# Moving the feed-forward steps in the hand-made order of an attention kernel: one turn, one linear and one statistics step each get another place

## The reference

```python
x = _layernorm(x + attention(x, w_qa, q_a_ln_w, w_qb, w_kva, kv_a_ln_w, w_kvb, w_o))   # 16 heads, causal
x = _layernorm(x + (einsum('bsi,oi->bso', x, weight * scale_weight[:, None]) + bias))
```

## Time and profile before

| | before |
|---|---|
| median of 3 runs | 1750.34 us (1749.48 to 1751.75) |
| the profiled execution | 1751.75 us |
| its span, first to last instruction | 1750.1 us |
| PE / PEld / DVE / ACT / POOL busy | 97 / 79 / 79 / 64 / 55 % |
| mean granted TensorE clock | 0.993 |

### The profile page before, as it was taken

One profiled execution on the slowest core, in us unless ns is written; L12 is line 12 of the kernel. 1 busy time (PEld: TensorE's weight loads), 2 busy tenths in 40 slices (PEclk: granted clock), 3 DMA queues, 4 the chain that ended last, 5 costly groups with the idle time before them and its releaser, 6 DMA issues.

```text
span 1750.1 us, 27869 instructions
## 1 busy us (share of the span) xinstructions
PE 1700.8 (97%) x8729; PEld 1390.7 (79%) x8729; DVE 1375.5 (79%) x2502; ACT 1122.8 (64%) x2133; POOL 963.3 (55%) x901
## 2 busy tenths in 40 slices
PE   7997899999999999999999999999999999999987
PEld 5565688888888888888888888888888888888554
DVE  3555787888888887878888888888888988888763
ACT  3553466675667576666667666766667766776763
POOL 3320355565565555555566555555655655665874
PEclk9998999999999999999999999999999999999999
DMA  6977221212311322223211412123113121113121
GB/s 200 344 284 244 63 79 58 82 55 87 130 55 61 115 67 67 80 66 128 79 55 49 133 55 91 55 70 127 58 55 127 45 65 43 43 43 108 56 91 67
DMA packets 111864, 165.28 MB, mean 94 GB/s; under 512 B 13488, under 2 KB 84144, under 8 KB 109424
## 3 DMA queue, kind: packets, MB, share of 16 engines
q1 hardware_dynamic: 105376, 124.03, 22.0%
q10 hardware_dynamic: 1728, 24.12, 3.3%
q0 software_dynamic: 4624, 15.47, 2.7%
HBM read 100.14 MB, written 63.44 MB: 93 GB/s over the span
## 4 chain that ended last, share of the span: by engine, by line
PE 88%; DVE 3%; DMA 3%; POOL 2%; issue 2%; ACT 2%; SPq 0%; DVEq 0%; ACTq 0%; POOLq 0%
PE rows L1406 35%; PE bank L1439 7%; PE bank L1436 7%; PE bank L1437 7%; PE rows L1469 6%; PE rows L1371 5%; PE bank L1469 3%; PE bank L1371 2%; PE rows L1384 2%; PE rows L351 2%; DMA cq_dram<-cq 2%; PE rows L1493 2%; PE bank L1426 2%; PE bank L1384 1%; PE rows L1415 1%
## 5 line engine op out<-in xcount | busy, mean ns | idle before, releaser
L1665 POOL TENSOR_TENSOR split_p<-pool,split_p 128x512 fp32r<-128x512 f32 x544 | 703.1, 1294 | 511.5 <-ACT split_p L1560 511.1
L1406 PE MATMUL rows<-q_c,key_c 128*128 128x512 f32 x1632 | 480.1, 403 | 5.0 <-DVE top L1784 4.7
L1548 ACT COPY pool<-rows 128x512 f32<-128x512 f32 x480 | 281.8, 587 | 237.8 <-PE rows L1406 237.1
L1799 DVE TENSOR_TENSOR pool<-bank,pool 128x512 f32<-128x512 f32 x544 | 370.0, 680 | 24.3 <-PE bank L1426 24.3
L1784 DVE TENSOR_TENSOR top<-rows,top 128x512 f32<-128x512 f32 x420 | 288.9, 688 | 126.9 <-ACT pool L1548 123.3
L1553 ACT ACTIVATE pool<-pool 128x512 f32<-128x512 f32 x544 | 345.9, 636 | 18.4 <-DVE pool L1799 17.7
L1560 ACT CAST split_p<-pool 128x512 fp32r<-128x512 f32 x544 | 333.2, 612 | 18.7 <-PE bank L1439 18.7
L1406 PE MATMUL rows<-q_pe,key_pe 128*128 128x512 f32 x1088 | 339.3, 393 | 3.9 <-DMA q_pe<-pe_dram 3.9
L1406 PEld LDWEIGHTS rows<-q_c,key_c 128*128 128x128 f32 x1632 | 290.4, 190 | 54.1 <-DVE top L1784 8.5
L1811 DVE TENSOR_TENSOR bank<-bank,pool 128x512 f32<-128x512 f32 x480 | 331.1, 690 | 0.0
L1406 PEld LDWEIGHTS rows<-q_pe,key_pe 128*128 128x128 f32 x1088 | 205.5, 189 | 50.1 <-DMA q_pe<-pe_dram 4.3
(11 more groups left out here) (190 smaller groups left out, 2131.5 us busy)
## 6 DMA issues: line engine op xcount, KB each, us to landing
q_pe<-pe_dram SPq DMA_DIRECT2D x128, 128.0 KB, 2.7
y_dram<-y SPq DMA_DIRECT2D x62, 256.0 KB, 2.0
cq<-cq_dram SPq DMA_DIRECT2D x20, 768.0 KB, 4.9
y<-y_dram SPq DMA_DIRECT2D x48, 256.0 KB, 3.0
wq_dram<-wq ACTq DMA_DIRECT2D x4, 2304.0 KB, 10.8
wo_dram<-wo ACTq DMA_DIRECT2D x4, 2048.0 KB, 10.1
pe_dram<-by_sin SPq DMA_DIRECT2D x32, 256.0 KB, 2.1
pe_dram<-by_cos SPq DMA_DIRECT2D x32, 256.0 KB, 2.1
```

Source lines behind the costliest of these rows:

```text
L1406: mm = pe.matmul(by_head(out), k, q, start=(z == 0), stop=(z == 4))
L1548: nc.scalar.copy(slot(n), SCORES[n % N_SCORES]).then_inc(scores_copied, 1)
L1665: nc.gpsimd.tensor_tensor(split_p[:, n % 2, 1, :], slot(n), stored(split_p[:, n % 2, 0, :]), ALU.subtract).then_inc(p_lo, 1)
L1799: nc.vector.tensor_tensor(slot(n), MAXES, slot(n), ALU.add).then_inc(shifted, 1)
```

## The change

The phases FFN_TURN and FFN_LINEAR go, and every FFN step has the one phase FFN, the last of a slot. `statistics`, `centre` and `invert` move from the head of slot n to its end. `turn` stays at n+1, behind `scale` and `add_bias` instead of ahead of them. `linear` moves from n+3 to n+2, `z_statistics` and `z_invert` from n+4 to n+3, `apply` and `out` from n+6 to n+5. Blocks below 14 may begin 10 slots behind their last `values` instead of 9; this moves blocks 12 to 15 from slots 567, 570, 572, 574 to 568, 571, 573, 575 and no other.

```diff
-SPREAD, SCORES_AT, COPIES, SHIFT, EXP, ROUND, VALUES, READ, MAX, USE_AT, FFN_TURN, FFN_LINEAR, FFN = range(13)
+SPREAD, SCORES_AT, COPIES, SHIFT, EXP, ROUND, VALUES, READ, MAX, USE_AT, FFN = range(11)
...
-        ready = last_value(output_of(u)) + (9 if u < DIRECT else 7)
+        ready = last_value(output_of(u)) + (10 if u < DIRECT else 7)
...
-        yield n, SPREAD, ("statistics", u)
-        yield n, SPREAD, ("centre", u)
-        yield n, SPREAD, ("invert", u)
-        yield n + 1, FFN_TURN, ("turn", u)
+        yield n, FFN, ("statistics", u)
+        yield n, FFN, ("centre", u)
+        yield n, FFN, ("invert", u)
         yield n + 1, FFN, ("scale", u)
         yield n + 1, FFN, ("add_bias", u)
-        yield n + 3, FFN_LINEAR, ("linear", u)
-        yield n + 4, FFN, ("z_statistics", u)
-        yield n + 4, FFN, ("z_invert", u)
-        yield n + 6, FFN, ("apply", u)
-        yield n + 6, FFN, ("out", u)
+        yield n + 1, FFN, ("turn", u)
+        yield n + 2, FFN, ("linear", u)
+        yield n + 3, FFN, ("z_statistics", u)
+        yield n + 3, FFN, ("z_invert", u)
+        yield n + 5, FFN, ("apply", u)
+        yield n + 5, FFN, ("out", u)
```

## The result

The changed kernel takes 1762.95 us (median of 4 executions, 1759.47 to 1763.8), the kernel before 1750.38 in the same job: a ratio of 1.0066, with an interval of 1.0051 to 1.0083. It is slower by 12.6 us, and the interval makes that 8.9 to 14.5 us. The forecast was 1755 and the range ended at 1760: the sign was right and the size was not.

What follows compares the result with a forecast made beforehand. PE was taken as the bound, POOL close behind; only waits could move. Terms -0.6 + 1.1 + 1.45 + 0.68 + 2.1 = +4.7 on 1751.75 gave 1756.5, less 1.4 for the median: 1755, range 1749.5 to 1760.

Steps and rivals of the forecast that it cites:

- The four gaps from `y` 62 to `linear` 15: Pauses ahead of `linear` 12, 13, 14 and 15, forecast to grow by 1.1, 1.45, 0.68 and 2.1 us.
- The two `o_hi` stalls: `copy_x` of blocks 7 and 9 queued behind `o_hi` on ACT, costing PE 1.7 and 2.8 us.
- The waits for `copy_out` of iterations 59 and 60: PE waits of 1.84 and 1.23 us, claimed to vanish because `linear` 5 and 7 hide the copy.
- the sum of the walk: Stretch up to the end of the last `y` (62), forecast 0.6 us shorter, bounds -5.1 and +2.
- Rival 1: Up to the last `y`, the two stalls are not met, so +0.2 us overall, 1750.5 us; chance 0.25.
- Rival 2: Earlier `linear` frees POOL and PE loses all 9.5 us of waits ahead of the last `y`: 1746.1 us; chance 0.06.
- The gap stays, so I leave the 1.76 us as they are: At `linear` 13, the lower-clock loss of 1.76 us was kept unchanged, with no added clock cost.
- Rival 3: All of `linear` 13 and 14 run at the lower clock, +5.1 us, 1760.2 us; chance 0.14.
- just hidden; that edit I cost at nothing: In ordinary pairs, the 0.68 us block copy was taken as hidden under one `values` of 0.68, costing 0.

Runs made afterwards that it cites:

- e5_busy: Changed kernel plus matmuls with overwritten results in PE's gaps ahead of `linear` 7 and 9, `turn` 13 and `linear` 13; 1756.91 us.
- e8_old_end: Changed kernel with the order and slots of the kernel before for blocks 12 to 15 only; 1754.93 us.
- e3_slots: Kernel before with `ready` at 10 slots instead of 9, so blocks 12 to 15 one slot later; 1753.34 us.
- e11_ahead_o_hi: Changed kernel with `copy_x` ahead of `o_hi` only, still behind `exp` and `hi`; 1757.36 us.
- e4_copy_first: Changed kernel with `copy_x` ahead of `exp`, `hi` and `o_hi` of its slot on ACT; 1754.43 us.
- e2_linear: Kernel before with only `linear`, `z_statistics`, `z_invert`, `apply` and `out` a slot earlier; 1790.14 us.
- e6_early: Kernel before with `statistics`, `centre` and `invert` of blocks 14 and 15 moved early, ahead of `z` 12 on DVE; 1748.01 us.
- e9_copy_ahead: e2_linear with one edit, `copy_x` sorted ahead of `centre` on ACT; 1756.86 us.

## Why the prediction was wrong in size

**Right.** The end was priced well. The four gaps from `y` 62 to `linear` 15 were forecast at 1.1 + 1.45 + 0.68 + 2.1 = 5.3 and measured 1.2 + 1.6 + 0.7 + 2.0 = 5.5, with the releasers named. The two `o_hi` stalls came where they were put: from the end of `linear` 6 to `linear` 7 4.8 us (forecast 4.8), from `linear` 8 to `linear` 9 5.8 (forecast 6.1). The waits for `copy_out` of iterations 59 and 60 went. But `linear` 12 was to begin 0.5 us later than before and began 5.6 later (1727.34 + 1.67 against 1723.39), so the sum of the walk failed ahead of the end. Rival 1, the middle that pays for the end, fell: both stalls are on the chain. Rival 2 fell too: `lo` was late for 0.9 us instead of 2.2, and PE had 10.7 us of new waits instead.

**The step that failed: the clock.** "The gap stays, so I leave the 1.76 us as they are" took the half-speed loss for a property of one gap that both kernels share. I had just put two new pauses ahead of `linear` 7 and 9 and did not ask what the clock would do behind them. The windows round `linear` 7 show it (the third number from the end is the clock):

```profile
1675.00:1677.40 2.40, 0.32 (x4) 0.11 (x2) 1.89 (x5) 1.61 (x4) 2.24 (x5) 1.00 0.06 24
1677.40:1679.00 1.60, 1.60 (x3) 0.76 (x4) 0.00 (x0) 1.60 (x4) 1.60 (x2) 0.63 0.00 0
1679.00:1681.00 2.00, 2.00 (x4) 0.86 (x3) 0.00 (x0) 1.50 (x3) 1.84 (x5) 0.50 0.02 7
1681.00:1683.00 2.00, 2.00 (x9) 0.92 (x7) 0.00 (x0) 0.32 (x1) 0.73 (x1) 0.95 0.76 255
```

Up to the end of the idle 2.08 us the clock is 1.00; in the `linear` behind them it is down to 0.50, the 1.2 GHz level, and it comes back within the same `linear`. A `linear` that waited takes 3.69 at full clock, so 7 and 9 lost 1.7 each, and 13 lost 6.67 - 5.21 - 0.24 = 1.2 more than before: 4.6 of the missing 7.4 us. e5_busy shows the cause: in its rows these 4.6 come back and the 5.21 - 3.45 = 1.76 that before lost as well, 6.3 in all.

The 3.4 of `linear` 7 and 9 are firmer than the 1.2 of `linear` 13. The first stand in both traces with these two waits, e8_old_end being the other. `linear` 13 is not fixed by its waits: behind the same wait of 3.0 us it took 5.21 in the kernel before, 5.93 in e3_slots and 5.98 in e8_old_end, and behind about 3.4 and 1.6 us 6.67 in the changed kernel, 6.16 in e11_ahead_o_hi and 5.26 in e4_copy_first:

```profile
1728.43 5.26 PE bank L1493 x8
```

Nor does a pause always cost the clock. In e2_linear five `linear` waited 2.4 to 3.1 us in the middle; three of them took 5.24 to 5.37, and two 3.67 at a clock of 1.00, one behind the longest wait of the five:

```profile
1656.91 3.67 PE L1493 MATMUL rows<-w_t,x_t 128*128 128x512 f32 x8 [3.11 <-ACT x_t L1611]
```

So that both new pauses would cost 1.7 us was not to be read from the kernel before. The fault of the prediction is that the clock behind `linear` 7 and 9 had neither a price nor a chance in it.

Rival 3 named the mechanism and looked for it at 13 and 14 only. `linear` 13 did run at the lower clock for nearly its whole length; `linear` 14, behind a wait of 0.77, ran at full clock. The rule of "TensorE: Matmul & The Clock Gate", Part 1, in the Trainium skill, that the lower rate is the default and work lifts it, spoke for the rival. e5_busy agrees, where more work kept the clock up; that a pause need not lower it (3.11 us above) the traces show beside it. In the Trainium skill "Perfetto Trace Analysis", section Matmul Optimizations, asks for matmuls back to back since the engine scales its power with its use; e5_busy agrees, its clock going from 0.97 and 0.90 to 1.00.

**The second step: "just hidden; that edit I cost at nothing".** The walk compared the 0.68 us of the copy with one `values` of 0.68 and took ACT to be free when `turn` ended. It is not. In the timeline of ACT in the changed kernel, ahead of `linear` 4:

```profile
1653.75 0.72 ACT L1605 ACTIVATE by_cos<-x_in,ffn_small 128x512 f32<-128x512 f32 x1 [0.53 <-DVE top L1853]
1654.38 0.61 ACT L1553 ACTIVATE pool<-pool 128x512 f32<-128x512 f32 x1
1654.90 0.60 ACT L1560 CAST split_p<-pool 128x512 fp32r<-128x512 f32 x1
1655.40 0.58 ACT L1611 COPY x_t<-rows 128x512 f32<-128x512 f32 x1
```

`scale`, `exp` and `hi` stand ahead of `copy_x`, and PE waits:

```profile
1656.12 3.67 PE L1493 MATMUL bank<-w_t,x_t 128*128 128x512 f32 x8 [0.66 <-ACT x_t L1611]
```

Of the 11 waits (10.7 us), those ahead of `linear` 7, 9, 12, 13, 14 and 15 are 2.08 + 2.01 + 0.77 + 1.57 + 0.77 + 1.55 = 8.75; the five others sum to 2.0. The traces of e4_copy_first and e11_ahead_o_hi put the price of `exp` and `hi` ahead of the copy at 1.9, which agrees.

**The sum.** The walk missed the end of `y` 62 by 5.0 us (-0.6 forecast, +4.4 measured). The ends of its `linear`, with 1.67 added, show where: `linear` 6 ends 1.8 us later than forecast, 7 3.7, 9 5.4 and 11 5.1. So 1.8 is from the small waits up to `linear` 6. The clock at 7 and 9 is 3.4, and 0.5 more is there because a `linear` behind a wait takes 3.69. Against that stand 0.3 that the stall ahead of 9 was overpriced and 0.3 behind it: 5.1 in all, the 5.0 to rounding. Behind `y` 62 the clock adds 1.2, and the `linear` that waited add 0.24 each at 12, 13, 14 and 15, since the first matmul behind a wait is longer on the chain: 1.0 that no step of the sum had. With 0.2 by which the four gaps were underpriced, 5.0 + 1.2 + 1.0 + 0.2 is the missing 7.4.

**What stays open.** Which pause lowers the clock and which does not is not shown, nor why `linear` 13 takes anything from 5.21 to 5.98 us behind the same chain. How often the drops at `linear` 7 and 9 come is known from two traces only.

## What to carry to other kernels

When steps of a fixed order are moved, write down for each step what stands ahead of it on its own engine and what that waits for: a step with ready inputs behind one that waits for a matmul closes a ring, and two halves of a change can each cost 24 and 39 us and together 13. A hiding place must be judged by the queue of the engine that does the hidden work, not by the length of the work that should cover it. And a new pause of TensorE can have a second price, the slower matmuls behind it, which here was nearly as large as the pause itself (1.7 us behind 2.0). It does not come each time, so it belongs in a forecast as a term with a chance, and one trace does not settle it.

## What the runs showed of the hardware

The granted clock fell from the 2.4 to the 1.2 GHz level behind an idle TensorE of 2.08 and of 2.01 us, and the full-speed clock was back within the same `linear`. The length of one pause did not decide: the clock stayed at 1.00 behind 1.84 us in the kernel before and behind 3.11 us in e2_linear, and behind two pauses of 1.1 and 1.23 us it fell in e6_early and stayed up in the kernel before. Executions of one kernel differ in it: of the ten of e9_copy_ahead the fastest took 1751.9 us at a whole-span clock of 0.996, and those at 0.991 and 0.992 took 1756.95 to 1758.34. A product of eight matmuls took 3.45 us on the chain and 3.69 behind a wait for its input, both at full clock. Extra matmuls whose result is overwritten, 16 as the page counts them (8745 against 8729), shortened the kernel by 6.3 us by the medians: with them the clock stayed at 1.00 in both windows of the tail.
